# Cross-attention with a routed FFN on one core: probabilities turned in 32x32 blocks by VectorE and moved through HBM, in place of TensorE transposes

## What is computed

```python
def xattn(latents, context, Wq, Wk, Wv, Wo):           # latents = layernorm(x), context = ctx_4096
    hidden = concatenate([context, latents], axis=1)   # 8 batches, 128 + 128 = 256 keys
    q = (latents @ Wq).reshape(b, 128, 4, 8, 128)      # 4 groups of keys x 8 heads of queries
    k = (hidden @ Wk).reshape(b, 256, 4, 128)
    v = (hidden @ Wv).reshape(b, 256, 4, 128)
    attn = softmax(einsum('bqhgd,bkhd->bhgqk', q, k) * 128 ** -0.5, axis=-1)
    return einsum('bhgqk,bkhd->bqhgd', attn, v).reshape(b, 128, 4096) @ Wo
x = x + xattn(layernorm(x), ctx_4096, ...)             # x is (8, 128, 512), fp32
x = x + ffn(layernorm(x))   # sign(weight) product, input and output scales routed by softmax over 8 experts
```

## Time and profile before

| | us |
|---|---|
| runs: median (lowest to highest) | 738.65 (737.88 to 739.76) |
| span of the profiled execution | 737.0 |
| PE busy | 725.1 (98%) |
| DVE busy | 400.4 (54%) |
| ACT busy | 363.7 (49%) |
| POOL busy | 266.6 (36%) |
| granted TensorE clock, mean | 1.000 of full speed (2.4 GHz) |
| bytes through DMA | 60.59 MB |

### The profile page before, as it was taken

One profiled execution on the slowest core, in us unless ns is written; L12 is line 12 of the kernel. 1 busy time (PEld: TensorE's weight loads), 2 busy tenths in 40 slices (PEclk: granted clock), 3 DMA queues, 4 the chain that ended last, 5 costly groups with the idle time before them and its releaser, 6 DMA issues.

```text
span 737.0 us, 11712 instructions
## 1 busy us (share of the span) xinstructions
PE 725.1 (98%) x3880; PEld 617.3 (84%) x3880; DVE 400.4 (54%) x742; ACT 363.7 (49%) x945; POOL 266.6 (36%) x316
## 2 busy tenths in 40 slices
PE   7999999999999999999999999999999999999996
PEld 5888888888888888888888888888888888888874
DVE  4552233664366436643664366436643664768876
ACT  3343324663466346634663466346634663465642
POOL 4243003441344134413441344134413441445554
PEclk9999999999999999999999999999999999999999
DMA  9566459110112320101223201012242010000001
GB/s 322 206 228 235 172 214 314 42 55 5 58 59 86 95 104 0 57 0 57 63 79 103 96 0 57 0 57 72 74 124 74 1 58 1 1 0 16 15 30 58
DMA packets 28418, 60.59 MB, mean 82 GB/s; under 512 B 2088, under 2 KB 2088, under 8 KB 27360
## 3 DMA queue, kind: packets, MB, share of 16 engines
q1 hardware_dynamic: 28384, 60.15, 24.0%
HBM read 41.27 MB, written 18.87 MB: 82 GB/s over the span
## 4 chain that ended last, share of the span: by engine, by line
PE 95%; DVE 2%; issue 1%; POOL 1%; DMA 1%; ACT 0%; SPq 0%; DVEq 0%; ACTq 0%; POOLq 0%
PE bank L947 48%; PE bank L1076 23%; PE bank L1059 12%; PE bank L1042 7%; PE bank L1158 1%; PE bank L1113 1%; DMA raw_a<-in_L_xattn_Wv 1%; PE bank L956 1%; DVE wq_pair L647 0%; PE bank L964 0%; PE bank L1105 0%; DVE stats L650 0%; PE bank L1128 0%; DVE acc L743 0%; PE bank L1091 0%
## 5 line engine op out<-in xcount | busy, mean ns | idle before, releaser
L351 POOL TENSOR_TENSOR prob<-prob,rsum 128x512 f32<-128x512 f32 x128 | 133.6, 1046 | 218.0 <-DVE rsum L731 218.0
L1076 PE MATMUL bank<-wo_pair,oT 128*128 128x512 f32 x768 | 203.5, 403 | 0.0
L947 PE MATMUL bank<-xT,wq_pair 128*128 128x512 f32 x768 | 184.0, 392 | 0.0
L947 PEld LDWEIGHTS bank<-xT,wq_pair 128*128 128x128 f32 x768 | 142.0, 188 | 28.8
L1076 PEld LDWEIGHTS bank<-wo_pair,oT 128*128 128x128 f32 x768 | 136.9, 188 | 24.8
L496 ACT ACTIVATE prob<-bank,nmax 128x256 f32<-128x256 f32 x256 | 118.6, 470 | 24.8 <-DVE nmax L725 24.8
L947 PEld LDWEIGHTS bank<-kg,qT 128*128 128x128 f32 x768 | 108.0, 189 | 9.5
L947 PE MATMUL bank<-kg,qT 128*128 128x256 f32 x768 | 112.7, 282 | 0.0
L313 POOL TENSOR_TENSOR wo_pair<-raw_b,wo_pair 128x512 fp32r<-128x512 f32 x32 | 41.0, 1312 | 189.2 <-ACT wo_pair L417 189.2
L417 ACT ACTIVATE pT<-bank 128x512 fp32r<-128x512 f32 x128 | 75.5, 597 | 59.2 <-PE bank L1042 59.2
L718 DVE SCALAR_TENSOR_TENSOR qT<-bank,qT 128x512 fp32r<-128x512 f32 x64 | 44.2, 691 | 107.8 <-ACT qT L487 107.8
(11 more groups left out here) (85 smaller groups left out, 576.7 us busy)
## 6 DMA issues: line engine op xcount, KB each, us to landing
v_park<-v_stage SPq DMA_DIRECT2D x8, 1024.0 KB, 4.3
raw_a<-in_L_xattn_Wq SPq DMA_DIRECT2D x8, 1024.0 KB, 6.8
raw_b<-in_L_xattn_Wo SPq DMA_DIRECT2D x8, 1024.0 KB, 5.4
k_park<-k_stage SPq DMA_DIRECT2D x8, 1024.0 KB, 3.9
kg<-k_park SPq DMA_DIRECT2D x32, 256.0 KB, 3.0
vg<-v_park SPq DMA_DIRECT2D x32, 256.0 KB, 3.2
craw<-in_ctx SPq DMA_DIRECT2D x8, 256.0 KB, 5.8
acc<-in_x SPq DMA_DIRECT2D x8, 256.0 KB, 5.9
```

The source lines that it names most:

```text
L351: nc.gpsimd.tensor_tensor(prob[:, p], prob[:, p], rsum[:, p].unsqueeze(2).to_broadcast([P, 2, KEYS]), ALU.mult).then_inc(prob_ready[p], 1)
L947: last = nc.tensor.matmul(dst, left(a, c), right(b, c), start=(n == 0), stop=(n == 3 * chunks - 1))
L1076: last = nc.tensor.matmul(wo_bank[:, :], oT[:, s, h, :], wo_pair[:, w, h, :], start=((s, w) == TERMS[0] and h == 0), stop=((s, w) == TERMS ...
```

## The change

Nothing of what is computed changes; the transposing of the probabilities does, and with it the order of all engines in the attention.

1. **Turn.** The PE transposes, `pt_half` and `pt_rest` are gone. DVE `turn` turns `prob[:, p]` (512 columns) in 32x32 blocks into `p_turned`. A block stays on its own 32 partitions, so the keys of a block row have to be moved to the right partitions: SP `park_p` writes `p_turned` (512 KB) into a scratch `p_park` in HBM, and after that has landed SP `fetch_p` reads it back with four DMAs (32 partitions x 4 x 256 elements each) into `p_low`.
2. **Split.** ACT `p_half` copies `p_low` (1024 columns, all four heads) to `p_high`, POOL `p_rest` subtracts in place. `attend` multiplies by `p_high` and `p_low`; its moving operand is now 4 runs of 128 columns. The key order of `k_stage`, and the column order in which `oT` is read out of the bank, follow.
3. **Lead.** `scores` are made three steps ahead (`LEAD = 3`), across the border of quads, so a step is now `attend(t)`, `scores(t+3, 0)`, one `q_unit` of the next quad, `scores(t+3, 1)`, `project_out(t)`.
4. **Other splits.** The LO of `wo_pair` moves from POOL to DVE (`wo_rest`, four in step 0 of a quad). The LO of `wq_pair` stays on POOL but goes by heads, in step 7 and steps 0 to 2 (`wq_rest`).
5. **Banks and tail.** The banks freed by the transposes serve the FFN; the tail is rewritten.

Core of the diff (unchanged lines around the pieces left out):

```diff
-            def transposes(g, qd, t, p):
-
-                pe.wait_ge(prob_ready[p], steps(g, qd, t + 1))
-                pe.wait_ge(pt_lo[p], steps(g, qd, t))
...
+            def turn(g, qd, t, p, first=False):
+
+                dve.wait_ge(prob_ready[p], steps(g, qd, t + 1))
+                if not first:
+                    dve.wait_ge(p_parked[t % 2], 16 * pairs(g, qd, t) - 16)
+                nc.vector.transpose(
+                    p_turned[:, t % 2, :, 2 * p:2 * p + 2, :].rearrange("p k h q -> p h k q"),
+                    prob[:, p].rearrange("p h (k e) -> p h k e", e=32)).then_inc(turned[p], 1)
...
+            def park_p(g, qd, t):
+
+                for p in range(2):
+                    sp.wait_ge(turned[p], steps(g, qd, t + 1))
+                sp.dma_start(p_park[t % 4], p_turned[:, t % 2].rearrange("p k h q -> p (k h q)")
+                             ).then_inc(p_parked[t % 2], 16)
+
+            def fetch_p(g, qd, t, first=False):
+
+                sp.wait_ge(p_parked[t % 2], 16 * pairs(g, qd, t))
+                if not first:
+                    sp.wait_ge(av_ready, steps(g, qd, t - 1))
+                rows = p_park[t % 4].rearrange("(i r) e -> r i e", r=32)
+                for j in range(QB):
+                    sp.dma_start(
+                        words(p_low[32 * j:32 * (j + 1), t % 2]).rearrange("r i c q -> r i (c q)"),
+                        rows[:, :, j * KC * QH * 32:(j + 1) * KC * QH * 32]).then_inc(p_in[t % 2], 16)
...
+            def p_half(g, qd, t):
+
+                act.wait_ge(p_in[t % 2], 16 * QB * pairs(g, qd, t))
+                copy(p_high[:, t % 2].rearrange("p i c q -> p (i c q)"),
+                     p_low[:, t % 2].bitcast(fp32).rearrange("p i c q -> p (i c q)")).then_inc(p_hi, 1)
...
+            def p_rest(g, qd, t):
+
+                pool.wait_ge(p_hi, steps(g, qd, t + 1))
+                part = p_low[:, t % 2].rearrange("p i c q -> p (i c q)")
+                nc.gpsimd.tensor_tensor(part, part.bitcast(fp32),
+                                        p_high[:, t % 2].rearrange("p i c q -> p (i c q)"),
+                                        ALU.subtract).then_inc(p_lo, 1)
...
+            def wo_rest(g, qd, h):
+
+                dve.wait_ge(wo_hi, count(g, QH, qd, h + 1))
+                subtract(wo_pair[:, LO, h, :], raw_b[:, h, :], wo_pair[:, HI, h, :]).then_inc(wo_lo, 1)
...
+            def step(g, qd, t, last):       # PE, without the FFN pieces of the last quad
+                attend(g, qd, t)
+                if ahead:
+                    scores(*ahead, 0)
+                if t == 0:
+                    q_unit(g, qd, UNITS - 1)
+                elif not final:
+                    q_unit(*quad_after(g, qd, 1), t - 1)
+                if ahead:
+                    scores(*ahead, 1)
+                project_out(g, qd, t, (0, 1))
+                project_out(g, qd, t, (2, 3))
...
+            def step(g, qd, t, last):       # ACT, without the FFN pieces
+                if not (final and t + 1 >= B):
+                    p_half(*step_after(g, qd, t, 1))
+                if t == 0:
+                    wo_half(g, qd, 0)
+                    wo_half(g, qd, 1)
+                o_half(g, qd, t)
+                if t == 0:
+                    wo_half(g, qd, 2)
+                    wo_half(g, qd, 3)
+                if ahead:
+                    exps(*ahead, 0)
+                if t == B - 1 and not last:
+                    wq_half(*quad_after(g, qd, 2), 0)
+                if t < QH - 1 and not final:
+                    wq_half(*quad_after(g, qd, 1), t + 1)
+                if t == 0:
+                    q_half(g, qd, UNITS - 1)
+                elif not final:
+                    q_half(*quad_after(g, qd, 1), t - 1)
+                if ahead:
+                    exps(*ahead, 1)
```

626 lines of the change are left out of this document (280 added, 346 removed).

## The result

The changed kernel takes 821.52 us (median of 4 runs, 819.47 to 822.95), the kernel before 738.83 beside it: ratio 1.112, interval 1.110 to 1.114. Slower was right; 754 was not, and 821.5 lies above the range. The profiled execution spans 819.7.

A forecast was written before the change was run, and what follows sets the result against it. PE, 95% of the chain, bounds the kernel. 737 less 55 (transposes), plus 7 (start), 55 (seven quads' waits), 11 (last quad), less 3 (PE being ahead) gave 752; 754 as the runs' median, range 712 to 798.

The forecast's parts named there:

- Slower: Whole kernel: the change makes it slower than the kernel before, 69 in 100.
- Removed work: PE: 128 pairs of transposes at 0.43 go, 55 us; a step's PE work falls to 8.3.
- Durations: New instructions: p_rest 2.35 on POOL, p_half 1.05 on ACT, turn 0.69 on DVE; attend's four runs cost nothing.
- Rival D: DVE's turn is held off by POOL: a step 10.5, a quad over 84, some 830; 6 in 100.
- Hand-off 7.3: Probabilities through HBM: write 2.6, four reads landing 2.8 after the last issue, with waits and issues 7.3; bounds 5.5 and 11.2.
- rival C: Hand-off through HBM is 9.3, slowed by small pieces or 1 MB loads ahead: a quad 80.4, 794; 17 in 100.
- loop 2: Two-step loop through normalise, turn, HBM hand-off, p_half, p_rest: 17.0 for two steps, 34.0 for steps 3 to 6.
- Loop 1, 9.0 with a piece of Wq: One-step loop through POOL, DVE's second turn and ACT: 7.7, or 9.0 with POOL's piece of wq_pair (steps 7, 0, 1, 2).
- Step 0, 13.1: Step 0 of a quad: DVE's four wo_rest wait for POOL, making 13.1 in place of 8.3; 10.5 without the wait.
- Loads "at nothing (1 a quad if not)": SP's loads of Wq, Wo, k and v end mostly before the next write: nothing, 1 a quad if not.
- Last quad, 11 lost: POOL's instructions take some 11 a step: 3 lost in steps 2 to 4, 5 in step 0, 3 in last three.
- Tail "as long as before": After the last quad: the tail takes as long as in the kernel before.

The follow-up runs named there:

- e1: Changed kernel with VectorE's turn of pair 0 moved behind the maximum of pair 1; median 768.87, ratio 1.043.
- e4: Changed kernel with each fetch reading what was parked two steps earlier, so no read waits for its own write; span 800.2.
- e2: Changed kernel with POOL's piece of Wq moved behind the normalising of pair 0; span 801.1.
- e3: Changed kernel with VectorE's four Wo subtractions reading a PSUM bank in place of raw_b, one SBUF input each; span 802.9.
- e17: Changed kernel with the loads of e13 alone: k and v over two quads, Wo and Wq in 256 KB pieces; span 810.4.
- e5: Changed kernel, last quad only: ACT's oscale_copy behind the next p_half; span 810.5.
- e6: Changed kernel, last quad only: POOL's normalising of pair 0 ahead of rstd and bias; span 814.8.
- e7: Changed kernel, last quad only: edits of e5 and e6, and PE's route transpose behind project_out; span 803.2.
- e13: On e1 with k/v loads spread, Wo subtractions behind o_rest and e7's edits: Wo, Wq loads in 256 KB pieces, at most three pieces a step; span 729.1.
- e16: The kernel of e13 again, timed in rounds; median 731.49, ratio 0.9907 to the kernel before.
- e12: On e13's base, without its load pieces: last quad's route transpose, channel scales, z and FFN product half a step later; span 737.6.
- e14: Edits of e12 and e13 together on their common base; median 734.81, ratio 0.994.
- e15: On e13: the last quad's router chain half a step later for the first three batches only; median 732.4, ratio 0.992.
- e8: On e1: the 1 MB loads of Wo and Wq in 256 KB pieces over steps 1 to 3 and 3 to 6; span 770.8.

## Why the prediction was wrong, step by step

- **Removed work.** Right: no transposes, and PE's own work of 8.3 a step shows wherever nothing holds it (8.28 in e1). So the four runs of `attend`'s operand, costed at nothing, did cost nothing that shows.
- **Durations.** Right, also p_rest (2.39 for 2.35) and the turn. Rival D is false: the turn is not held by POOL. That its 830 lies nearest to the measured time is luck.
- **Hand-off 7.3.** 8.0 measured in one step: SP 0.07 behind the turn's end at 406.61, and p_half starting at 414.57. Short of rival C's 9.3; e4 confirms loop 2 and its place. In steps 3 to 6 of quads 0, 2 and 4 the miss was 0.5 to 0.7 of 34. Sound.

```profile
406.68 0.32 SPq L298 DMA_DIRECT2D p_park<-p_turned  x1
414.57 1.06 ACT L491 ACTIVATE p_high<-p_low 128x1024 fp32r<-128x1024 f32 x1 [1.14 <-DMA p_low<-p_park]
```

- **Loop 1, 9.0 with a piece of Wq.** Mis-sized, 9.7: I took POOL's piece as ready and did not look at where ACT makes its HI. Three steps a quad (7, 1 and 2), together about 1.8 a quad, seven quads: 13. That the loop itself runs as I wrote it, e1 and e2 show.
- **Step 0, 13.1.** The port wait is shown by e3, but half of the path was another, and that 13.0 was met is in part luck. I had the second subtraction wait for POOL's piece of Wq; it took 0.64, and POOL instead stood 4.0 for ACT's HI of Wq (both in the rows under e3). Two entries of my path, 3.7 and 6.1, also lie above what its own rows give, about 3.4 and 5.2; with these it is 12.2.
- **Loads "at nothing (1 a quad if not)".** Wrong where k and v are loaded: steps 3 to 6 of quads 1, 3 and 5 lie 2.2 to 2.7 above 34, together 7.5, and e17 took back 9.3 in all. Quad 6, with the load of the FFN weights and VectorE's work on them, lies 4.4 above; the sum had neither. A load of 1 MB behind a fetch lies ahead of the next park. I had written that it would end mostly before the next write and not worked out the bytes of such a step.
- **Last quad, 11 lost.** The step that failed most: by the estimate above some 31 of the 67.7, with 16.6 in steps 2 to 4. I summed POOL's instructions for one step (11) and took them as the loop. The loop was longer: through `oscale_copy` ahead of p_half on ACT, and the gate and routes behind the turn on VectorE, to a transpose in the middle of `project_out`. e5 and e6 took 8.5 and 4.3 off steps 2 to 6, e7 12.2. A part of these steps ran at the lower clock (0.52 from 754.0 to 757.3), and no run parts it from the loop. I had costed the last three steps at 3 lost and not looked at the FFN product that moved into them.
- **Tail "as long as before".** Wrong by 7.5, with one FFN product less in it and the granted clock at 0.73 for 0.99. In e13 and e16 the clock was 0.66 and 0.73 with 29.0 and 27.7 us of tail. That waits of TensorE pull its clock down fits all of these, but no run changed the clock alone, so how much of the 7.5 is clock and how much order stays open.
- **Rivals and range.** All of them varied the seven quads; none varied the last quad or the tail, where over half of the miss lay, and so 798 was too low. The prediction names the instruction that closes both loops, VectorE's second turn, but no rival put a price on its place (e1).

Left open: why the last steps of e12, e14 and e15 lengthened, since one of e15's did so at full clock, and how the 15 us or so of steps 5 to 7 of the last quad part into moved work, waits and clock.

## What to carry to other kernels

Before a transfer or a slower engine is put into a pipelined step, walk each in-order queue once and write down the closed loops, the prologue's and the last stage's too, and look for the instruction that waits with others behind it: moving that one was worth 53 us here by the medians, and all later edits together 37 (768.9 to 731.5). Small cyclic transfers share a queue with large loads at a price: cut the loads into pieces, count the bytes of the fullest step, and put the pieces where there is room; the pieces alone gave nothing (e8). Gains of removed waits need not add (715 by the sum, 739 measured), so run the combination.

## What I had not expected of the hardware

- A 32x32 block turn of 128x512 fp32 on VectorE takes 0.71, and 0.72 beside a POOL subtraction of 2.41 (386.53 and 386.45).
- A 512 KB write to HBM lands after 2.6 us in the median and after 5.77 behind a 1 MB load issued 2.9 us earlier.
- A two-operand SBUF subtraction on VectorE lasts until POOL's instruction beside it ends and 0.55 more: 2.76 at 373.65 beside a p_rest that ends at 375.86, and 0.64 at 376.95 without one.
- At the same instruction count the granted clock of the whole run went from 0.95 (changed kernel) to 0.98 (e16) as TensorE's waits went; eight matmuls of an FFN product took 3.76 in one tail (clock 0.50) and 2.09 in the other.
